# Counting edges by pairs of tiles in two buffer sets, ScalarE making one of two destination one-hots, with the 50 destination ranges written out

## What is computed

```python
row, col, norm = _gcn_norm(edge_index, n)
xs = [x]
h = x
for _ in range(K):
    h = jax.ops.segment_sum(norm[:, None] * h[col], row, num_segments=n)
    xs.append(h)
```

## Time and profile before

| | us |
|---|---|
| median of three runs | 4544.77 |
| lowest, highest | 4540.06, 4547.14 |
| the profiled execution | 4547.42 |
| its span | 4545.9 |
| TensorE busy | 2962.5 |
| VectorE busy | 2218.4 |
| ScalarE busy | 370.0 |

### The profile page before, as it was taken

How to read it: one execution, slowest core, us unless ns; L and a number is a source line. 1 busy time by engine, 2 the same in 40 slices (tenths; PEclk the granted TensorE clock), 3 DMA queues, 4 the chain that set the end, 5 groups by cost and what they waited for, 6 DMA issues and landing times. The chain is left out here.

```text
span 4545.9 us, 68833 instructions
## 1 busy us (share of the span) xinstructions
PE 2962.5 (65%) x16813; PEld 1910.2 (42%) x16939; DVE 2218.4 (49%) x5486; ACT 370.0 (8%) x793; POOL 977.4 (21%) x985
## 2 busy tenths in 40 slices
PE   1467677563066765602777628923999999989476
PEld 1133333352054454501555426712656565656345
DVE  7465656587356664712444420065444444444463
ACT  0211111100000000000000012212000000000131
POOL 0000000076367700566774020020000000000000
PEclk9888989876589898756999959966999999999797
DMA  1200000253134411623553153223121212121101
GB/s 60 69 29 36 32 32 32 103 194 118 30 107 119 116 27 54 204 65 111 140 140 93 59 202 125 101 65 135 57 94 57 93 57 93 57 94 57 37 0 40
DMA packets 206513, 378.78 MB, mean 83 GB/s; under 512 B 35807, under 2 KB 155344, under 8 KB 203222
## 3 DMA queue, kind: packets, MB, share of 16 engines
q1 hardware_dynamic: 120090, 188.27, 11.9%
q0 software_dynamic: 50384, 139.33, 10.9%
q10 hardware_dynamic: 35968, 50.35, 3.2%
HBM read 270.37 MB, written 108.29 MB: 83 GB/s over the span
## 5 line engine op out<-in xcount | busy, mean ns | idle before, releaser
L1850 PE MATMUL hop_wide<-hop_hs,counts 128*128 128x512 bf16 x3000 | 990.9, 381 | 35.0 <-DMA hop_hs<-hop_parts 35.0
L1851 PE MATMUL hop_narrow<-hop_hs,counts 128*128 128x256 bf16 x3125 | 855.8, 274 | 170.6 <-DMA hop_hs<-hop_parts 155.5
L653 POOL DMA_INDIRECT gat_ring<-hx_rows,src_i x784 | 793.4, 1012 | 339.3 <-issue 211.2
L1850 PEld LDWEIGHTS hop_wide<-hop_hs,counts 128*128 (+1 forms) x3125 | 307.1, 98 | 577.9 <-issue 215.5
L888 PE MATMUL cnt_acc<-cnt_oh_src,cnt_oh_dst 128*128 x1764 | 407.0, 367 | 137.3 <-issue 71.5
L1241 PE MATMUL agg_acc<-agg_msg,agg_oh 128*128 x880 | 278.3, 444 | 126.4 <-DVE agg_oh L1180 125.9
L888 PEld LDWEIGHTS cnt_acc<-cnt_oh_src,cnt_oh_dst 128*128 x1764 | 180.5, 102 | 350.8 <-issue 292.6
L1851 PEld LDWEIGHTS hop_narrow<-hop_hs,counts 128*128 (+1 forms) x3125 | 307.2, 98 | 36.4
L1823 DVE TENSOR_SCALAR hop_h<-hop_narrow,all_dis 128x256 f32<-128x256 f32 x125 | 60.5, 484 | 527.2 <-PE hop_narrow L1851 527.2
L1241 PE MATMUL agg_acc<-gat_ring,agg_oh 128*128 x880 | 258.4, 417 | 89.0 <-DVE agg_oh L1177 89.0
L848 DVE TENSOR_SCALAR cnt_oh_src<-cnt_number,cnt_column 128x1600 f16 x441 | 277.6, 629 | 0.0
(11 more groups left out here) (408 smaller groups left out, 3557.6 us busy)
## 6 DMA issues: line engine op xcount, KB each, us to landing
look_part<-src_low SPq DMA_DIRECT2D x28, 896.0 KB, 4.9
hop_hs<-hop_parts POOLq DMA_DIRECT2D x25, 960.0 KB, 8.1
hop_parts<-hop_parts SPq DMA_DIRECT2D x125, 192.0 KB, 1.9
count_rows<-cnt_out SPq DMA_DIRECT2D x50, 400.0 KB, 2.4
counts<-count_rows ACTq DMA_DIRECT2D x5, 4000.0 KB, 35.2
exp_w<-in_L_ffn_w SPq DMA_DIRECT2D x16, 1024.0 KB
hop_acc<-x_gcn SPq DMA_DIRECT2D x125, 128.0 KB, 2.0
x_gcn<-hop_acc SPq DMA_DIRECT2D x125, 128.0 KB, 1.8
```

The costliest lines, as they stand in the source:

```text
L653: pool.indirect_dma_start(out=self.ring[:, t % RING, :], out_offset=None, in_=self.g.hx_rows, in_offset=bass.IndirectOffsetOnAxis(ap=self. ...
L1850: pe.matmul(wide[i][:, :], count, hs[:, t, 0:2 * D], start=(t == 0), stop=(t == NB - 1))
L1851: mm = pe.matmul(narrow[i][:, 0:D], count, hs[:, t, 2 * D:3 * D], start=(t == 0), stop=(t == NB - 1))
```

## The change

Each engine's work in `counts` is rewritten, and the graph tables get one more tensor, `window_pairs`, the bounds halved to pairs of tiles.

- The unit of work becomes a pair of tiles (2p, 2p+1). A range visits the pairs from the one with its first edge to the one with its last, so a pair in which two ranges meet is visited in both. Buffers for the even tiles (k = 0) and for the odd tiles (k = 1) are separate sets, with two slots each and a `hot` and `used` semaphore each.
- ScalarE makes the destination one-hot of the even tiles, in two dependent instructions: |node - half the row number + key| by `Abs` into `apart`, then 1 - 2 times that by `Relu`. The rows it starts from, `nodes`, are one more ScalarE instruction for each range. VectorE makes the destination one-hot of the odd tiles and both source one-hots.
- TensorE waits for `hot[0]` and `hot_a`, runs four matmuls, waits for `hot[1]` and runs four more.
- The loops over ranges are gone on TensorE, VectorE and ScalarE: the 50 ranges stand in the program one after the other, with constants for all that depends on the range. Only the upper bound of a range is read, and handed to the next as its lower one. On TensorE the read now stands behind the four starting matmuls; on VectorE and ScalarE within the first visit of a range or just ahead of it.
- ScalarE empties a set of banks with one instruction over four banks, placed between the first visit of the next range and the rest of that range's visits.

```diff
+                link(nc.vector.tensor_scalar(g.window_pairs[:, :], g.window_tiles[:, :], 1, None, ALU.logical_shift_right))
...
-        DEPTH = 4
...
-        oh_src = s.sb("oh_src", [P, DEPTH, HALF], F16)
-        oh_dst = s.sb("oh_dst", [P, DEPTH, P], F16)
+        oh_src = [s.sb(f"oh_src{k}", [P, 2, HALF], F16) for k in range(2)]
+        oh_dst = [s.sb(f"oh_dst{k}", [P, 2, P], F16) for k in range(2)]
+        minus_half, nodes, apart = s.sb("minus_half", [P, P]), s.sb("nodes", [P, 2, P]), s.sb("apart", [P, 2, P])
+        hot_a, numbered_a, far = s.sem("hot_a"), s.sem("numbered_a"), s.sem("far")
...
-        hot, used = s.sem("hot"), s.sem("used")
+        hot, used = ([s.sem(f"{n}{k}") for k in range(2)] for n in ("hot", "used"))
...
+        def last_pair(eng, w):
+
+            return eng.value_load(g.window_pairs[0:1, w + 1:w + 2], min_val=0, max_val=ET // 2 - 1)
...
+                def visit(p, w, then=None):
+
+                    for k in range(2):
+                        dve.wait_ge(used[k], after(p + w))
+                        if k:
+                            dve.tensor_scalar(at(oh_dst[k], (p + w) % 2), half16[:, :], at(key, 2 * p + k),
+                                              minus_first[:, w:w + 1], ALU.subtract, ALU.is_equal)
+                        dve.tensor_scalar(at(oh_src[k], (p + w) % 2), number[:, :], at(column, 2 * p + k), None,
+                                          ALU.is_equal).then_inc(hot[k], 1)
+                        if then and not k:
+                            found = then()
+                    return found if then else None
+
+                first = 0
+                for w in range(NW):
+                    last = visit(first, w, lambda: last_pair(dve, w))
                     with dve.If(last > first):
-                        with dve.Fori(first + 1, last + 1) as t:
-                            step(t, w)
-
-                with dve.Fori(0, NW) as w:
-                    window(w)
+                        with dve.Fori(first + 1, last + 1) as p:
+                            visit(p, w)
+                    first = last
...
-                        for n in range(BANKS):
-                            act.activation(out[i][:, n * COLS:(n + 1) * COLS], acc[i][n][:, 0:COLS],
-                                           ACT.Copy).then_inc(read[i], 1)
+                act.wait_ge(ready, after(1))
+
+                def visit(p, w):
+                    slot = (p + w) % 2
+                    act.wait_ge(used[0], after(p + w))
+                    act.activation(at(apart, slot), nodes[:, w % 2, :], ACT.Abs, bias=at(key, 2 * p)).then_inc(far, 1)
+                    act.wait_ge(far, after(p + w + 1))
+                    act.activation(at(oh_dst[0], slot), at(apart, slot), ACT.Relu, scale=-2.0,
+                                   bias=g.ones[:, 0:1]).then_inc(hot_a, 1)
+
+                def evict(w):
+                    i, j = w % 2, w // 2
+                    act.wait_ge(summed[i], after(j + 1))
+                    act.wait_ge(stored[i], after(16 * j))
+                    act.activation(out[i][:, :].rearrange("p (n c) -> p n c", n=BANKS), whole[i][:, :, 0:COLS],
+                                   ACT.Copy).then_inc(read[i], 1)
+
+                first = 0
+                for w in range(NW):
+                    act.activation(nodes[:, w % 2, :], minus_half[:, :], ACT.Identity, bias=minus_first[:, w:w + 1]
+                                   ).then_inc(numbered_a, 1)
+                    last = last_pair(act, w)
+                    act.wait_ge(numbered_a, after(w + 1))
+                    visit(first, w)
+                    if w:
+                        evict(w - 1)
+                    with act.If(last > first):
+                        with act.Fori(first + 1, last + 1) as p:
+                            visit(p, w)
+                    first = last
+                evict(NW - 1)
...
-                def window(w, i, j):
-                    first, last = bounds(pe, w)
-                    pe.wait_ge(read[i], after(BANKS * j))
+                first = 0
+                for w in range(NW):
+                    i, j = w % 2, w // 2
+                    pe.wait_ge(read[i], after(j))
                     for n in range(BANKS):
                         pe.matmul(acc[i][n][:, 0:1], zero16[:, 0:P], zero16[:, 0:1], start=True, stop=False,
                                   skip_group_check=True)
-                    with pe.Fori(first, last + 1) as t:
-                        pe.wait_ge(hot, after(t + w + 1))
-                        for n in range(BANKS):
-                            mm = pe.matmul(acc[i][n][:, 0:COLS], at(oh_dst, (t + w) % DEPTH),
-                                           oh_src[:, bass.ds((t + w) % DEPTH, 1), n * COLS:(n + 1) * COLS].rearrange(
-                                               "p a f -> p (a f)"), start=False, stop=False, skip_group_check=True)
-                        mm.then_inc(used, 1)
+                    last = last_pair(pe, w)
+                    with pe.Fori(first, last + 1) as p:
+                        for k in range(2):
+                            pe.wait_ge(hot[k], after(p + w + 1))
+                            if not k:
+                                pe.wait_ge(hot_a, after(p + w + 1))
+                            for n in range(BANKS):
+                                mm = pe.matmul(acc[i][n][:, 0:COLS], at(oh_dst[k], (p + w) % 2),
+                                               at(oh_src[k], (p + w) % 2)[:, n * COLS:(n + 1) * COLS],
+                                               start=False, stop=False, skip_group_check=True)
+                            mm.then_inc(used[k], 1)
```

More of the change, by code:

```diff
@@ L895, in window @@
                     mm.then_inc(summed[i], 1)
-                with pe.Fori(0, NW // 2) as j:
-                    for i in range(2):
-                        window(2 * j + i, i, j)
+                    first = last
 def edge_weights(nc, g, io, layer):
```

27 lines of the change are left out of this document (7 added, 20 removed).

## The result

| | before | after |
|---|---|---|
| median of four runs, us | 4544.41 | 4412.99 |
| lowest, highest, us | 4540.06, 4547.14 | 4410.15, 4418.66 |
| span of the profiled execution, us | 4545.9 | 4417.1 |

The ratio is 0.971 (95% interval 0.970 to 0.973): 131 us less, where 88 were forecast. The time lies 44 us under the forecast and 5 under the low end of its range.

A forecast was written before the change was run, and what follows sets the result against it. TensorE's instruction queue was taken to bound the counting stage. Visits and changes of range -102 us, stall +12, start +1.7 gave -88; 4547.4 - 88 - 2.6 = 4457 us, range 4418 to 4515.

The forecast's parts named there:

- What bounds the kernel: Counting stage, 606 us before: TensorE's instruction queue sets the whole pace, also at the lower clock.
- The pair's price: TensorE's visit of two tiles: 1.18 + 0.40 + 0.24 + 0.08 = 1.90 us, bounds 1.71 and 2.13, 245 visits.
- The join: Between a pair's two fours of matmuls on TensorE: a wait and new addresses, 0.24 us, bounds 0.13 and 0.40.
- The second wait: TensorE's wait for ScalarE's one-hot ahead of the first four matmuls: one more queue instruction, 0.08 us.
- Changes of range: TensorE between ranges: one bound read and the outer loop gone, 0.76 us each for 49, against a mean of 1.73.
- The stall behind the eviction: A range's second visit, TensorE waiting for ScalarE's one-hot queued behind the eviction: 0.25 us for each of 49, 12 us.
- The first rival: ScalarE late after each eviction: stall of 0.8 to 1.4 us for 49 ranges, say 4495 us; chance 0.15.
- the start: First visit waits for ScalarE's shifted row, 1.2 us, plus 0.5 for graph tables and semaphores: 1.7 us.
- a better clock brings nothing: Counting stage: pairs' matmuls fit into 1.90 us at 2.4 GHz, and the slots cover the lag at 1.2 GHz.
- A pair that shares nothing: Rival on TensorE's visits: the join costs as much as a visit's gap, a pair 2.44 us, 4588 us; chance 0.04.
- ScalarE as the pace: Rival in the counting: ScalarE sets the pace; at 2.3 us a visit the kernel takes 4600 us; chance 0.03.
- Code coming late: Rival: written-out ranges stall on instruction fetches, 2.4 us in every range adding 120 us, 4577; chance 0.03.

The follow-up runs named there:

- The single tiles written out: Kernel before with its 50 ranges written out, each reading one bound; single tiles in four slots kept: stage 545.1 us, ratio to before 0.989.
- the rolled pairs: Changed kernel with ranges back in a loop of 25 turns, two ranges each, both bounds read: stage 515.4 us, ratio to before 0.988.

## Why the prediction came out as it did

*What bounds the kernel.* Right. The queue of TensorE was the bound and still is: with half the array's work a visit stays at 1.76, with two instructions more it grows by both of them.

*The pair's price.* This term failed, and with it 245 x (1.90 - 1.75) = 37 of the 44 us. The second four matmuls were put at 0.40 + 0.24 = 0.64 us of queue time, and the traces show 0.44 to 0.48 for them between the fourth load and the loop's branch. The join was put at 0.24 us from the aggregation's register instructions; it is 0.14, 0.10 less. And the visit was built from distances between loads, as if the gap of 0.65 us stood behind the last load of a pair too. But the second four loads come at the array's pace (0.17) while the queue is already at 0.12 a load and in the loop's branch. Between first and last load the forecast had 0.41 + 0.24 + 0.40 = 1.05 us, the trace has 1.03; from the last load to the next visit it had 0.85, the trace has 0.69 to 0.72. The sum has to be made in the queue's instructions. The second wait is no part of the error: without it a visit is 0.07 us shorter, and 0.08 was forecast.

*Changes of range.* Right in kind, 0.62 against 0.76: 49 x 0.14 = 7 us of the miss, which with the 37 makes the 44. (For the stage the forecast had 503 + 12 = 515 us, and 470 came; ahead of it and behind it small differences cancel.) The single tiles written out show 0.62 by themselves.

*The stall behind the eviction.* Right in place, and in what it waits for. That the size agrees (49 x 0.25 = 12 us, forecast 12) is luck. The forecast had the one-hot ready 2.57 us after the last matmul and asked for after 2.58, and added 0.25 us for ranges at the lower clock. But in the change only the first 5 us ran at the lower clock, ahead of any change of range. In the trace the one-hot is ready after 403.95 - 401.61 = 2.34 us, and TensorE would have asked 0.28 us before that, after 2.06; so both times were put too late, and the second by more. The first rival, 0.8 us and more, did not come. What the forecast did not ask is whether ScalarE's help pays: VectorE was said to have 1.54 us against 1.90, which already meant that it needed no help. Its one-hot costs the stage 31 us.

*The start and the clock.* The forecast had 1.7 us for the start; the first load stands at 230.8 us, and before at 231.6, so it cost nothing. The clock went from 0.91 to 0.99 in the stage. For single tiles the forecast was right that the lower clock costs nothing: in the kernel before, the 61 visits wholly at 1.2 GHz took 1.18 us in the mean, and so did the 277 wholly at 2.4. For pairs its step "a better clock brings nothing" failed: in the rolled pairs, 42 us at 1.2 GHz cost 9 us, which the slots did not cover. In the change it is about 1 us, as only 5 us were at that clock. How much the change would lose at the 0.91 of before no run shows; at the rolled pairs' rate 85 us at 1.2 GHz would cost some 18, an estimate.

*The other rivals.* A pair that shares nothing (2.44) and ScalarE as the pace (2.3) are refuted by 1.72. Code coming late: 97 packets against 71, and no stall in the visits or the changes. All 49 visits with a change of range lie between 2.33 and 2.58 us, and behind the first range no other visit takes over 2.11; a fetch of 2.4 us would stand out. The forecast took from the Trainium skill (Advanced Engine Details and Errata, ISA Cache) that two lines of 256 instructions are held. The same list gives TensorE 128 KB where it gives 32 KB otherwise, and it does not say that a loop across an edge is fetched anew in each turn; that was the forecast's own step, and no such stall is in this trace. The Trainium skill's price of about 108 ns for a compare-and-branch (Advanced Engine Details and Errata, Control Flow Timing) is half of what the pair loop's branch takes here, 208 ns when taken.

*The range.* With a pair's low bound (1.71) the sum reached 4410, below the low end of 4418: the bounds of the one term that carries 245 visits were not taken into the range in full.

## What to carry to other kernels

Where an engine waits for "issue", count the instructions of its queue and not the distances of its visible work: waits, addresses in registers, the loop's branch. Look first whether the distances are the array's own, as they were at 1.2 GHz. Group work until the array's time exceeds the queue's, and keep buffer addresses fixed so that the queue can run ahead; here this was worth 61 us of the stage beyond the change. Before an engine takes over work from one that is not the bound, ask what its semaphore costs the one that is.

## What the runs showed of the hardware

A register load from SBUF on TensorE's queue takes 0.30 us, and a median of 0.64 (up to 0.75) when a 400 KB transfer from SBUF runs beside it; without the transfer 0.30 again. A wait more on TensorE's queue cost 0.11 us where it was an instruction of its own; two waits can share one. With fixed addresses the queue needs almost no register instructions, and the weight loads come 0.169 us apart without a break through branches and changes of range. The granted clock fell to 1.2 GHz for 290 of 462 us when the matmuls had half the columns at the same rate of instructions, where in the change, with all columns, it was 2.4 GHz but for the first 5 us. At 1.2 GHz weight loads of 400-column matmuls stand 0.34 us apart, at 2.4 GHz 0.17; single-tile visits of 1.18 us, bound by the queue, did not change with it, visits of two tiles went from 1.74 to as much as 2.52. Two 128x1600 one-hots in a row on VectorE take 1.18 us, although each lasts 0.63.
